# One read-out for each of the last two rows of the fifth sweep: the diagonal block joins its row's group

## The reference, cut to what matters

```
layer 0:  u = tanh([x, t] W1 + b1) W2 + b2 + adj (x B') - rowsum(adj) (x B')
layer 1:  T1 = adj x;  T2 = 2 adj T1 - x;  T3 = 2 adj T2 - T1;  out = sum of Tk weights[k]
layer 2:  h = (adj x + x) / (deg + 1);  out = normalize(relu([x, h] W + b))
layer 3:  w = mask(adj) * 0.5 ** (rank of the last 100 entries of a row);  out = w (x W) + b
```

## Time and profile before

| | |
|---|---|
| median of 3 runs | 3071.27 us (3069.88 to 3072.64) |
| the profiled execution | 3075.36 us, its span 3073.4 us |
| PE busy | 2939.1 us, 96% of the span |
| DVE busy | 2816.7 us, 92% |
| ACT busy | 2362.4 us, 77% |
| the transfers of adj | 1143.02 MB, 95.0% of 16 engines' time |
| mean granted TensorE clock | 0.993 |

### The profile page before, as it was taken

The page is one execution under the profiler, slowest core; times in us unless marked ns, Lnnn a source line. Parts: engine busy times, 40 slices in busy tenths (PEclk is TensorE's granted clock), DMA queues, the critical chain, the costliest instruction groups (busy, mean ns, idle before and its releaser), DMA issues.

```text
span 3073.4 us, 35291 instructions
## 1 busy us (share of the span) xinstructions
PE 2939.1 (96%) x13488; PEld 2160.7 (70%) x13488; DVE 2816.7 (92%) x2383; ACT 2362.4 (77%) x1635; POOL 13.2 (0%) x31
## 2 busy tenths in 40 slices
PE   7999999999899998999989999998989999999998
PEld 6667778787788886888867888776666555555554
DVE  7999988988998889998899988999999899999997
ACT  5787877777877778776777776877787888888887
POOL 0000000000000000000000000000000000000000
PEclk9999999999999999999999999999999999999999
DMA  9999988999999999999999999989999999999996
GB/s 343 382 400 382 388 351 349 367 362 357 367 396 384 378 375 383 396 383 380 377 372 370 382 377 377 379 340 352 389 403 408 357 383 384 383 386 384 382 384 250
DMA packets 158934, 1148.17 MB, mean 374 GB/s; under 512 B 18016, under 2 KB 18256, under 8 KB 19504
## 3 DMA queue, kind: packets, MB, share of 16 engines
q1 hardware_dynamic: 157312, 1143.02, 95.0%
q0 software_dynamic: 1088, 2.48, 0.2%
q10 hardware_dynamic: 368, 0.43, 0.0%
HBM read 1143.75 MB, written 2.10 MB: 373 GB/s over the span
## 4 chain that ended last, share of the span: by engine, by line
PE 68%; DVE 23%; DMA 4%; ACT 3%; issue 2%; SPq 0%; ACTq 0%; DVEq 0%
PE ACC L916 26%; DVE lo L646 18%; PE ACC L923 15%; PE ACC L1032 14%; DMA raw<-in_at 4%; PE PSF L1046 4%; PE PST L1046 4%; ACT hi L454 2%; DVE SV L752 1%; PE PSF L989 1%; PE PST L939 1%; PE PSF L1012 1%; PE PSF L992 1%; PE PSF L987 0%; DVE SV L759 0%
## 5 line engine op out<-in xcount | busy, mean ns | idle before, releaser
L646 DVE TENSOR_TENSOR lo<-raw,hi 128x2048 fp32r<-128x2048 f32 x832 | 1879.2, 2287 | 151.4 <-ACT hi L454 145.8
L454 ACT CAST hi<-raw 128x2048 fp32r<-128x2048 f32 x832 | 1585.2, 1912 | 525.2 <-PE ACC L916 306.7
L916 PE MATMUL ACC<-hi,T 128*128 128x512 f32 x4992 | 1281.7, 394 | 6.5 <-DVE T L604 4.3
L916 PEld LDWEIGHTS ACC<-hi,T 128*128 128x128 f32 x4992 | 936.4, 189 | 209.1 <-DVE T L604 4.6
L923 PE MATMUL ACC<-lo,T 128*128 128x512 f32 x3200 | 889.6, 400 | 95.6 <-DVE lo L646 88.8
L923 PEld LDWEIGHTS ACC<-lo,T 128*128 128x128 f32 x3200 | 589.0, 189 | 296.2 <-DVE lo L646 182.3
L661 DVE SCALAR_TENSOR_TENSOR M<-raw,M 128x512 bf16<-128x512 f32 x1008 | 637.0, 687 | 42.7 <-PE ACC L1032 26.0
L460 ACT ACTIVATE Wf<-ACC,w_bias 128x1024 fp32r<-128x1024 f32 x512 | 568.0, 1114 | 130.3 <-PE ACC L1032 129.7
L1032 PE MATMUL ACC<-M,rank_b 128*128 128x512 bf16 x2032 | 529.9, 383 | 8.2 <-ACT Wf L460 4.6
L1032 PEld LDWEIGHTS ACC<-M,rank_b 128*128 128x128 bf16 x2032 | 159.0, 98 | 267.0 <-issue 132.1
L1046 PE MATMUL PST<-Wf,S 128*128 128x512 f32 x512 | 210.1, 491 | 0.0
(11 more groups left out here) (162 smaller groups left out, 988.0 us busy)
## 6 DMA issues: line engine op xcount, KB each, us to landing
raw<-in_at SPq DMA_DIRECT2D x1088, 1024.0 KB, 6.9
SV<-in_x_cols SPq DMA_DIRECT2D x8, 256.0 KB, 13.0
out<-O POOLq DMA_DIRECT2D x7, 256.0 KB, 6.6
out<-O ACTq DMA_DIRECT2D x1, 256.0 KB, 2.0
w_sb<-in_w POOLq DMA_DIRECT2D x3, 64.0 KB, 9.3
bias<-in_bias_rows ACTq DMA_DIRECT2D x1, 128.0 KB, 9.8
l1w_sb<-in_l_w POOLq DMA_DIRECT2D x2, 64.0 KB, 8.4
rank_f<-in_rank_mats POOLq DMA_DIRECT2D x1, 128.0 KB, 9.9
```

What stands on the lines that cost most here:

```text
L454: nc.scalar.copy(hi[:, c % NH], raw[:, c % NR]).then_inc(hi_done, 1)
L646: tt(lo[:, c % NR], raw[:, c % NR], hi[:, c % NH].bitcast(f32), ALU.subtract).then_inc(lo_done, 1)
L916: ins = mm(acc[:, part], w, hi[:, p.c % NH, s, part], start=p.opens and s == 0 and i == 0, stop=False)
```

## The change

In sweep 5 the diagonal blocks of rows 6 and 7 are no longer groups of their own. Each is taken at the head of its row's group, which is then called M: the order ends "P3 P4 P5 M6 M7". An M group has one accumulator and one read-out, that of a D group: ACT takes one half of the partitions and DVE the other for row 6, ACT alone all 128 for row 7. It is put at c+2 for row 6, and at c for row 7, ahead of `tx`. No blocks and no matmuls are added or taken away.

Since four pairs go from before P4 to before P6 and four from before P5 to before P7, rows end elsewhere: row 4 at 751 (755 before), row 5 at 771 (779), row 6 at 799 (803), rows 3 and 7 at 735 and 831 as before. Every step of a tail moves with its row's end, and where steps of two rows meet at one number, the older row's comes first. The two `st` go from 735 and 755 to 771 and 799.

```diff
-        order = "D2 D1 D0 D3 D4 P1 D5 P2 P3 D6 P4 D7 P5 P6 P7"
+        order = "D2 D1 D0 D3 D4 P1 D5 P2 P3 P4 P5 M6 M7"
     for name in order.split():
         r = int(name[1:])
-        out.append((name[0], r, [blocks[r]] if name[0] == "D" else blocks[:r]))
+        out.append((name[0], r, ([blocks[r]] if name[0] in "DM" else []) + (blocks[:r] if name[0] in "PM" else [])))
...
+        if kind == "M":
+            due("ACT", c - NP * (r + 1), "st", k, r)
+            due("ACT", c + 2 if r < NB - 1 else c, "diag", k, r)
+            if r < NB - 1:
+                due("DVE", c + 2, "diag", k, r)
...
-            if r:
+            if kind == "P":
                 due("DVE", c + 2, "sum", k, r)
...
-            due("DVE", c + 1, "sum", k, r)
             due("PE", c + 3, "comb", k, r)
...
-        if kind == "D":
+        if kind in "DM":
             return [(sv_act, act_sv["diag", k, r])] + ([(sv_dve, dve_sv["diag", k, r])] if r < NB - 1 else [])
...
-                    act.wait_ge(pair_done, group_end[k, "D", r] + 1)
-                    nc.scalar.copy(SV[part, cols(I)], ACC[acc_of[k, "D", r]][part, :]).then_inc(sv_act, 1)
+                    kind = diag_kind[k, r]
+                    act.wait_ge(pair_done, group_end[k, kind, r] + 1)
+                    nc.scalar.copy(SV[part, cols(I)], ACC[acc_of[k, kind, r]][part, :]).then_inc(sv_act, 1)
```

More of the change, by code:

```diff
@@ L196, in graph_layers @@
     last_acc = acc_of[group_order[-1]]
+    diag_kind = {(k, r): kind for k, kind, r in group_order if kind in "DM"}
     row_no = {}
@@ L749, in step @@
                 elif what == "diag":
-                    dve.wait_ge(pair_done, group_end[k, "D", r] + 1)
+                    kind = diag_kind[k, r]
+                    dve.wait_ge(pair_done, group_end[k, kind, r] + 1)
                     dve.wait_ge(sv_act, sv_kept(k - 1, I))
-                    tt(SV[u, cols(I)], SV[u, cols(I)], ACC[acc_of[k, "D", r]][u, :], ALU.add).then_inc(sv_dve, 1)
+                    tt(SV[u, cols(I)], SV[u, cols(I)], ACC[acc_of[k, kind, r]][u, :], ALU.add).then_inc(sv_dve, 1)
                 elif what == "sum":
@@ L978, in step @@
                         pe.wait_ge(sv_act, act_sv["diag", k, r])
-                        pe.wait_ge(sv_dve, dve_sv["sum" if r else "diag", k, r])
+                        for last_sum in ("sum", "diag"):
+                            if (last_sum, k, r) in dve_sv:
+                                pe.wait_ge(sv_dve, dve_sv[last_sum, k, r])
+                                break
                     if k == 5:
```

## The result

The changed kernel takes 3084.78 us (median of 6 runs, 3083.5 to 3086.81) where the kernel before takes 3071.32 (6 runs, 3066.55 to 3073.28): the ratio is 1.0041, 95% interval 1.0031 to 1.0051, or 13 us more. The forecast was 3074.7 us with a range up to 3080.0, so the time lies outside it. The profiled execution of the changed kernel took 3085.49 us, its span 3083.5.

A forecast was written before the change was run, and what follows sets the result against it. Sweep 5 was taken as bound by DVE, with transfers close behind, the last stage by PE. The terms, -1.1 + 0.9 + 1.7 + 1.9 = +3.4 us on 3071.27, gave 3074.7 us; range 3069.0 to 3080.0.

The forecast's parts named there:

- Term 1: Sweep 5, pairs 742 to 743: row 6's DVE read-out of D6 goes, -1.1 us (ends -1.2 and 0).
- Term 2: Rows 3 to 5: l3w and comb meet at 753, PE waits 3.2 us; +0.9 us (ends -1 and +5).
- Rival B: Wait at 753 stops six slots being freed and PE's clock can fall: +9.2 us, 3080.5 us; chance 0.20.
- Term 3: Gaps of 28 and 32 ahead of rows 6 and 7: six pairs at DMA's pace, +1.7 us (0 to +2.2).
- Term 4: Seam to the last stage: row 7's copy precedes tx and table load, rank(2) later by +1.9 us (ends 0, +1.9).
- Rival D: ACT pays the table load's 1.28 us once more before its first exponential: +4.7 us, 3076.0 us; chance 0.08.

The follow-up runs named there:

- e2: The kernel before with only row 3's l3w, s_hi and s_lo four pairs later, so l3w meets the next comb at 757: 3081.5 us, ratio 1.0035.
- the repeat: The changed kernel itself measured once more, unaltered, beside new runs of the kernel before: 3082.5 us, ratio 1.0041.
- e4: The kernel before with only row 6's diagonal block merged; row 4 ends at 751, row 7 keeps its own group: 3078.3 us, ratio 1.0025.
- e6: The changed kernel with row 3's tt and l3w at 751 and its s_hi and s_lo at 753: 3076.2 us, ratio 1.0017.
- e1: The changed kernel with the tails of rows 4 to 6 and row 6's read-out at their old pair numbers: 3075.2 us, ratio 1.0015.
- e7: The changed kernel with row 7's tx, then a one-column exponential loading the table, ahead of row 7's copy: 3076.4 us, ratio 1.0021.
- e8: e6 with the seam of e7 (tx and table load ahead of row 7's copy): 3071.4 us, ratio 1.0005.
- e9: e1 with the seam of e7 (tx and table load ahead of row 7's copy): 3069.4 us, ratio 0.9997.
- e10: The changed kernel with the exponential's table loaded ahead of row 7's copy, tx staying behind the copy: 3078.6 us, ratio 1.0027.
- e5: The changed kernel plus an unused transpose of 16 matmuls on PE between row 3's l3w and row 4's comb: 3078.4 us, ratio 1.0023.
- e3: The kernel before with only row 7's diagonal block merged; row 4 ends at 755: 3076.1 us, ratio 1.0017.
- e12: e3 with the seam repaired (tx and table load ahead of row 7's copy): 3071.2 us, ratio 0.9999.

## Why the prediction was wrong, step by step

**Term 1, D6's read-out: right.** It was forecast at -1.1; `lo` of 744 starts 1.24 us sooner relative to 736.

**Term 2, the gap of 16: the step that failed.** The mechanism was right in each link, and e2 shows it alone: `comb` behind `l3w` at one number, PE's wait for `s_lo` (3.2 forecast, 2.38 and 3.27 in two profiles), `fin_a` and `hi` of 757 late. The term was mis-sized: +0.9 was forecast, and between the pairs 752 and 772 the profile loses 8.3 us (8.0 in the repeat). In the medians, each against its own runs of before, the collision is worth 7.1 us (e4), 8.4 (e6), 9.5 (e1) and 10.4 (e2), and with the seam repaired 4.2 and 7.0 (e7 against e8 and e9). The step said "PE stands still for 8.5 - 5.3 = 3.2 us, and then runs `comb` for 2153.4 - 2149.9 = 3.5 us". It took a duration from a stretch at full clock and used it behind a wait. `comb` took 6.3 us (6.1 to 6.8 in the six profiles with the wait unfilled), the first matmuls behind it 0.9 more, and DVE's waits behind it came to 7.5 us and not 3.6. That is 3.9 us of the missing 7.4, and the longer `comb` (2.8 us) and matmuls (0.9) make nearly all of it. The rest lies in small things: the wait of 1.13 us ahead of `lo` of 753, which was not forecast, about 1 us of DVE's work that now falls into this stretch, and the old waits. Of these 2.9 us were set against the new ones and did go (0.55 + 1.00 + 0.34 + 1.00 between the pairs 752 and 764), but 0.55 + 1.00 come back between 764 and 772 with row 4's `l3w`, where the step had allowed +0.2. The term's upper end of +5 was built with full-clock durations as well, so the range missed it.

**Rival B named it and priced it low.** It gave the halved clock 3.4 to 3.6 us of time and 1.7 us of cost, from one fall in the trace of before. The fall here lasted 10.2 us in the changed kernel, in e2, e4, e7 and e10, and 13.6 in the repeat. Its 3080.5 would have been the better forecast, still 4 us low.

**Term 3, the transfers' pace: mechanism right, size too large.** In the changed kernel ahead of row 6's end the transfers set the pace as forecast:

```profile
2253.93 1.91 ACT L460 CAST hi<-raw 128x2048 fp32r<-128x2048 f32 x1 [0.58 <-DMA raw<-in_at]
2256.41 1.91 ACT L460 CAST hi<-raw 128x2048 fp32r<-128x2048 f32 x1 [0.57 <-DMA raw<-in_at]
2258.90 1.91 ACT L460 CAST hi<-raw 128x2048 fp32r<-128x2048 f32 x1 [0.58 <-DMA raw<-in_at]
```

They are 2.48 us apart. But the +1.7 did not come. From pair 772, behind row 5's end, to pair 831 seven profiles have both long gaps (the changed kernel, its repeat, e5 to e8 and e10); against the one profile of before they take between 0.9 us less and 1.5 more, +0.1 on average. e3 and e12, which have the gap of 32 alone, take 2.5 and 1.5 us more there, and e12 is no slower than before in the median. No run took the term alone.

**Term 4, the seam: right in place, half in size.** It was forecast at +1.9 from copy, `tx` and table; `rank(2)` came 2.0 us later against `lo` of 831, and 1.9 in the repeat. The clock behind this wait added 1.7 us in the first profile and none in the repeat. In the medians the seam costs 5.2 us (e3 against e12), 5.7 (e1 against e9) and 4.1 (e6 against e8), each against its own runs of before; the traces show 1.9 to 3.6 us of it, and 0.4 more that the repair wins. Where the rest lies stays open. Rival D is refuted: in the rows of the seam above the exponential at 2356.30 follows the table load, which ends at 2356.29, at once.

## What to carry to other kernels

In a schedule written by pair numbers, list after every shift which steps of two rows now share a number and one buffer; one such meeting cost more than all the read-outs saved. Price what stands behind a new wait of PE at half clock too, as the 32 small matmuls of `comb` here: 3.5 us at full clock, 6.1 to 6.8 behind the wait. And when a read-out moves to another engine, look at what was queued there under cover of the old order, a table load above all.

## What the runs showed of the hardware that was not expected

After PE's wait of 2.4 to 3.8 us ahead of `comb`'s 32 small matmuls the granted clock stayed at 1.2 GHz for 10 to 14 us, in all six profiles in which the wait was there unfilled, though PE was busy again. With 2 us of the wait filled it was 7 us, and the fall came after PE had already worked at 2.4 GHz for 2.7 us. The Trainium skill (TensorE: Matmul & The Clock Gate, HAM oscillation) warns that gaps on PE bring the half clock. The traces agree in kind, with 0.68 of the clock granted from 2140 to 2156 behind the 2.38 us, though the gaps of that section are longer than this one.

The wait's length alone does not tell what follows. At the seam a wait of 2.38 us stands ahead of `rank` in six profiles; in three of them (the changed kernel, e3, e6) the clock fell for 3.4 us at its end, in the other three (the repeat, e1, e5) not at all. The two waits of 2.1 us further on were both followed by the half clock in ten profiles of fourteen, and neither was in three. What makes the low stretch at pair 753 three to four times as long is not shown: there `l3w` and `comb`, 48 small matmuls, stand in a row around the wait, and no run has them in a row without a wait.
